# Row maxima of attention scores as y + relu(x - y): one reduction of 1024 or 2 x 512 scores becomes a relu on ScalarE and a fused add and maximum on VectorE

## The reference

```python
scores = einsum('bqhd,bkhd->bhqk', q, k) / sqrt(16)
probs = softmax(scores, axis=-1)          # over 1024 keys
out = einsum('bhqk,bkhd->bqhd', probs, v)
```

## Time and profile before

| what | value |
|---|---|
| median of 3 runs | 438.49 us (438.16 to 438.51) |
| the profiled execution's own time | 436.62 us |
| its span | 434.8 us |
| granted clock of TensorE, mean | 0.985 |
| PE busy | 420.0 us (97%) |
| DVE busy | 370.9 us (85%) |
| ACT busy | 310.1 us (71%) |
| POOL busy | 138.3 us (32%) |

### The profile page before, as it was taken

The page is one execution under the profiler, slowest core; times in us unless marked ns, Lnnn a source line. Parts: engine busy times, 40 slices in busy tenths (PEclk is TensorE's granted clock), DMA queues, the critical chain, the costliest instruction groups (busy, mean ns, idle before and its releaser), DMA issues.

```text
span 434.8 us, 8295 instructions
## 1 busy us (share of the span) xinstructions
PE 420.0 (97%) x3153; PEld 182.1 (42%) x3153; DVE 370.9 (85%) x613; ACT 310.1 (71%) x612; POOL 138.3 (32%) x195
## 2 busy tenths in 40 slices
PE   7999999998999999999999999999999999899993
PEld 3647333333444344444444444444434444333330
DVE  5844798998999999999999999999999999623443
ACT  2231111227889889999999899999989989766882
POOL 7972332444004030511313040322304030401554
PEclk9999999997899999999999999999999999999997
DMA  8949995444000010000000000000000000020002
GB/s 261 310 107 127 133 120 84 62 75 73 4 2 2 21 39 3 2 2 2 4 2 2 2 2 4 2 3 0 3 4 2 3 0 4 3 87 2 21 23 67
DMA packets 13624, 18.09 MB, mean 42 GB/s; under 512 B 3168, under 2 KB 7552, under 8 KB 13584
## 3 DMA queue, kind: packets, MB, share of 16 engines
q1 hardware_dynamic: 12064, 16.44, 20.0%
q10 hardware_dynamic: 1520, 1.12, 0.9%
HBM read 6.72 MB, written 2.10 MB: 20 GB/s over the span
## 4 chain that ended last, share of the span: by engine, by line
PE 86%; POOL 3%; DVE 3%; issue 2%; ACT 2%; DMA 2%; SPq 0%; DVEq 0%; POOLq 0%; ACTq 0%
PE st L1122 32%; PE oT L1090 27%; PE st L934 6%; PE sm L1197 3%; PE oT L1173 3%; PE oT L934 3%; PE sm L1038 2%; PE sm L1013 2%; PE sm L1099 2%; DMA x_sb<-in_x 2%; PE st L1154 2%; PE st L963 2%; POOL arena L466 1%; DVE negmax L795 1%; PE sm L1203 1%
## 5 line engine op out<-in xcount | busy, mean ns | idle before, releaser
L803 DVE TENSOR_REDUCE neghalf<-sm 128x1 f32<-128x512 f32 x448 | 270.9, 680 | 1.5 <-PE sm L1013 1.2
L709 ACT ACTIVATE arena<-st 128x512 f32<-128x512 f32 x448 | 233.0, 600 | 21.1 <-PE st L1122 16.4
L1013 PE MATMUL sm<-kA,qA 48*128 48x512 f32 x448 | 158.1, 446 | 0.0
L1122 PE MATMUL st<-qA,kA 50*128 50x512 f32 x448 | 154.9, 442 | 1.4 <-DVE z_sb L846 1.1
L1090 PE MATMUL oT<-arena,vg 128*32 128x256 f32 (+3 forms) x1568 | 129.7, 423 | 0.0
L1122 PEld LDWEIGHTS st<-qA,kA 50*128 50x128 f32 x448 | 74.0, 186 | 98.7 <-ACT arena L709 82.1
L537 POOL TENSOR_TENSOR rsum<-junk,consts 128x16 f32<-128x16 f32 x13 | 37.9, 2913 | 127.9 <-ACT junk L681 127.9
L1013 PEld LDWEIGHTS sm<-kA,qA 48*128 48x128 f32 x448 | 74.1, 186 | 2.6 <-DVE neghalf L803 2.1
L1090 PEld LDWEIGHTS oT<-arena,vg 128*32 128x32 f32 x1568 | 33.5, 109 | 46.7 <-issue 42.4
L795 DVE TENSOR_REDUCE negmax<-sm 128x1 f32<-128x1024 f32 x32 | 37.9, 1218 | 7.0 <-PE sm L1038 7.0
L730 ACT ACTIVATE arena<-st 128x512 f32<-128x512 f32 x48 | 27.0, 602 | 14.6 <-PE st L1154 14.6
(11 more groups left out here) (122 smaller groups left out, 360.2 us busy)
## 6 DMA issues: line engine op xcount, KB each, us to landing
qA<-arena SPq DMA_DIRECT2D x45, 128.0 KB, 5.1
x_sb<-in_x SPq DMA_DIRECT2D x8, 256.0 KB, 5.8
kA<-qA SPq DMA_DIRECT2D x12, 128.0 KB, 6.6
wT_sb<-in_wT SPq DMA_DIRECT2D x1, 1024.0 KB, 7.5
out<-x_sb SPq DMA_DIRECT2D x1, 896.0 KB, 4.1
out<-x_sb SPq DMA_DIRECT2D x4, 224.0 KB, 2.0
z_sb<-in_wq SPq DMA_DIRECT2D x1, 768.0 KB, 10.0
qA<-qA SPq DMA_DIRECT2D x3, 128.0 KB, 3.8
```

The source lines that it names most:

```text
L709: act.activation(probs[:, s % PB, h, :], st[:, st_score(0, s, h) % 3, :], ACT.Exp, scale=float(D) ** -0.5).then_inc(st_free, 1)
L803: dve.tensor_reduce(neghalf[:, e // 16, e % 16, j % 2:j % 2 + 1], sm[:, n % 4, :], AX.X, ALU.max, negate=True).then_inc(sm_free, count)
L1013: pe.matmul(sm[:, n % 4, :], qA[rows, half, g // 2, h, qt * P:(qt + 1) * P], kA[rows, g // 2, kh * HALF:(kh + 1) * HALF], start=True, stop ...
L1122: pe.matmul(st[:, n % 3, :], kA[rows, g // 2, kt * P:(kt + 1) * P], qA[rows, half, g // 2, h, :], start=True, stop=True).then_inc(st_full, 1)
```

## The change

A row tile's two halves of keys give scores x and y. The kernel after computes the maximum of the two, element by element, as y + relu(x - y). x - y comes from one matmul of the queries with the difference of the two halves of k. ScalarE takes relu of that bank and writes it to SBUF; one VectorE instruction (`tensor_tensor_reduce`) adds it to the bank of y and takes the maximum along the row.

All 32 row tiles of group 0 go this way (`first_relu`, `first_row_max`). In the loop the row tiles that begin at j mod 32 = 12 and 24 do (`BY_RELU`), four of 32 per group; the other 28 are two reductions each, as before.

What comes with it: the differences of k are made by GpSimd (one subtraction, one low part) and ScalarE (one high part), put in place for group 0 by `put_rows("rows of d", 0)` instead of `put_rows("rows of k", 0)`, and brought to `d_rows` by six DMAs. Maxima are kept with their own sign (`row_top`, `half_top`), and the constant rows in `kA` are -1 in place of 1. The relus lie in tiles 4 and 5 of `x_sb`, which two DMAs load again from `x` after the last maximum. `late_gate` and `late_heads` change places. In ScalarE's list the casts, the squares and the tanhs of the mixed stretch are put between the relus.

```diff
+BY_RELU = (12, 24)
+def by_relu(j):
+    return j % 32 in BY_RELU
# ScalarE, mixed stretch
+            def first_relu(e):
+                act.wait_ge(sm_full, 2 * e + 1)
+                if e >= 2:
+                    act.wait_ge(sm_free, 2 * (e - 1))
+                act.activation(relus[:, e % 2, :], sm[:, 2 * e % 4, :], ACT.Relu).then_inc(relu_done, 1)
...
+            for kind, i, rows in MIXED:
+                if kind == "v":
+                    cast(waiting)
+                    waiting = None
+                for r in range(rows):
+                    if r == 2 and waiting is not None:
+                        cast(waiting)
+                        waiting = None
+                    first_relu(entry)
+                    entry += 1
+                    if kind == "q" and i[0] == 3 and r == 1:
+                        gate_tanh_of(i[1])
...
# ScalarE, loop
+            def row_relu(g, j):
+                n = relus_through(g, j) - 1
+                act.wait_ge(sm_full, sm_score(g - 1, j) + 1)
...
+                act.activation(relus[:, n % 2, :], sm[:, sm_score(g - 1, j) % 4, :], ACT.Relu).then_inc(relu_done, 1)
                         act.activation(probs[:, s % PB, h, :], st[:, st_score(0, s, h) % 3, :], ACT.Exp,
                                        scale=float(D) ** -0.5).then_inc(st_free, 1)
+                        if by_relu(4 * s + h - 1):
+                            row_relu(g + 1, 4 * s + h - 1)
# VectorE
+            def top_of_sum(to, bank, n):
+                dve.wait_ge(relu_done, n + 1)
+                return dve.tensor_tensor_reduce(relus[:, n % 2, :], bank, relus[:, n % 2, :], 1.0, LOWEST,
+                                                ALU.add, ALU.max, to)
+            def pair_max(g, j):
+                n, e = sm_score(g, j), j // 2
                 dve.wait_ge(sm_full, n + 2)
+                top_of_sum(half_top[:, e // 16, e % 16, 0:1], sm[:, (n + 1) % 4, :],
+                           relus_through(g + 1, j) - 1).then_inc(sm_free, 1)
...
                 for j in range(64):
                     if j == 33:
                         both_halves(g, 0)
-                    row_max(g, j, 2 if j in (OUT1_AT - 1, OUT0_AT - 1) else 1)
+                    if by_relu(j):
+                        pair_max(g, j)
+                    elif not by_relu(j - 1):
+                        row_max(g, j, 2 if by_relu(j + 1) or j in (OUT1_AT - 1, OUT0_AT - 1) else 1)
# TensorE, loop
+                keys = d_rows[rows, g // 2, :] if by_relu(j) else kA[rows, g // 2, kh * HALF:(kh + 1) * HALF]
...
+                    if i >= 4 and by_relu(i - 4):
+                        pe.wait_ge(relu_done, relus_through(g + 1, i - 4))
                     score_rows(g + 1, i, sm_score(g, i), 2 if first and i == OUT1_AT - 1 else 1)
# GpSimd
+                if (halves[n]) == ("k", 1):
+                    pool.tensor_tensor(difference, rotated_at(0), rotated_at(n), ALU.subtract).then_inc(diff_done, 1)
                 if n < len(halves) - 3:
                     rope_sum(n + 1)
+                if (halves[n]) == ("k", 1):
+                    pool.wait_ge(diff_hi, 1)
+                    pool.tensor_tensor(difference_part(1), difference, difference_part(0).bitcast(F32),
+                                       ALU.subtract).then_inc(diff_lo, 1)
# TensorE, mixed stretch
                 if e == 0:
-                    pe.wait_ge(pj_act, emptied(PJ_AT["rows of k", 1])[1])
+                    pe.wait_ge(pj_act, emptied(PJ_AT["rows of d", 0])[1])
```

More of the change, by code:

```diff
@@ L132, in sm_score, with relus_through @@
     return sm_base(g) + j + (1 if j >= OUT1_AT else 0) + (1 if j >= OUT0_AT else 0)
+def by_relu(j):
+    return j % 32 in BY_RELU
+def relus_through(g, j):
+    return 32 + len(BY_RELU) * (2 * (g - 1) + j // 32) + sum(b <= j % 32 for b in BY_RELU)
 def sm_out1(g):
@@ L608, in cast, with put_k @@
                     act.wait_ge(stacked[n - PART_BUFS], 16 * SLOT_DMAS)
-                act.activation(part(n, 0), rot[:, n % 2, :], ACT.Copy).then_inc(part1, 1)
-            def put_k(i):
-                e = PJ_AT["rows of k", i]
+                act.activation(part(n, 0), rotated_at(n), ACT.Copy).then_inc(part1, 1)
+            def put_k(what, i):
+                e = PJ_AT[what, i]
                 act.wait_ge(pj_full, e + 1)
@@ L623, in put_q, with keep_u @@
                     act.activation(qA[0:ROWS + KR, 0, 0, h, :], pj(e)[0:ROWS + KR, :], ACT.Copy).then_inc(pj_act, 1)
[L625 to L638, removed]
+            def keep_u(hh):
+                e = PJ_AT["u", hh]
+                act.wait_ge(ffn_in, 80)
+                act.wait_ge(pj_full, e + 1)
+                act.activation(uT[:, hh * HALF:(hh + 1) * HALF], pj(e), ACT.Copy,
+                               scale=p_sb[:, 0:1]).then_inc(pj_act, 1)
+            def first_relu(e):
[3 more added lines that the diff above has]
+                act.activation(relus[:, e % 2, :], sm[:, 2 * e % 4, :], ACT.Relu).then_inc(relu_done, 1)
             def gate_tanh_of(t):
@@ L657, in squares @@
                                accum_out=norms[:, t, 0:1]).then_inc(norm_done, 1)
[L659 to L668, removed]
+            for n in range(3):
+                cast(n)
+            put_q()
+            act.wait_ge(diff_done, 1)
+            act.activation(difference_part(0), difference, ACT.Copy).then_inc(diff_hi, 1)
+            cast(3)
+            put_k("rows of k", 1)
+            put_k("rows of d", 0)
+            entry, waiting = 0, None
+            for kind, i, rows in MIXED:
[10 more added lines that the diff above has]
+                        gate_tanh_of(i[1])
+                if kind == "q":
+                    waiting = halves.index((kind, i))
+                elif waiting is not None:
+                    cast(waiting)
+                    waiting = None
+                if kind == "u":
+                    keep_u(i)
+                if kind == "z":
+                    squares(i)
+                if (kind, i) == ("z", 1):
+                    act.wait_ge(pj_full, PJ_AT["max0", 0] + 1)
+                    act.activation(maxT[:, 0, :], pj(PJ_AT["max0", 0]).bitcast(BF16)[0:32, 0:P],
+                                   ACT.Copy).then_inc(pj_act, 1)
             def evacuate(blocks, half, free):
@@ L674, in evacuate @@
                     act.wait_ge(*free)
-                act.activation(heads[:, half, :], oT[:, :], ACT.Copy).then_inc(heads_out, 1)
+                act.activation(heads[half], oT[:, :], ACT.Copy).then_inc(heads_out, 1)
             def copy_turned(n, at):
@@ L969, in put_rows @@
                 n = PJ_AT[kind, i]
-                of = halves.index(("k", i) if kind == "rows of k" else ("q", (0, 0)))
-                column = 0 if kind == "rows of k" else 1 + i
+                column = 1 + i if kind == "rows of q" else 0
                 claim(n)
                 pe.wait_ge(columns_set, 1 + 3 * len(Q_SLOTS))
-                for which, done in ((0, part1), (1, part2)):
-                    pe.wait_ge(done, of + 1)
-                    mm = pe.matmul(pj(n), put_col[:, which, column, :],
-                                   part(of, which), start=(which == 0), stop=(which == 1))
+                for which in range(PARTS):
+                    if kind == "rows of d":
+                        pe.wait_ge((diff_hi, diff_lo)[which], 1)
+                        of_which = difference_part(which)
+                    else:
+                        of = halves.index(("k", i) if kind == "rows of k" else ("q", (0, 0)))
+                        pe.wait_ge((part1, part2)[which], of + 1)
+                        of_which = part(of, which)
+                    mm = pe.matmul(pj(n), put_col[:, which, column, :], of_which, start=(which == 0), stop=(which == 1))
                 mm.then_inc(pj_full, 1)
@@ L1098, in turn_heads @@
                 for t in range(TH):
-                    mm = pe.transpose(bank[:, t * P:(t + 1) * P], heads[:, half, t * P:(t + 1) * P], id_sb[:, :])
+                    mm = pe.transpose(bank[:, t * P:(t + 1) * P], heads[half][:, t * P:(t + 1) * P], id_sb[:, :])
                 return mm
```

101 lines of the change are left out of this document (70 added, 31 removed).

## The result

The kernel after takes 464.21 us (median of 4 runs, 463.81 to 465.42), the kernel before beside it 438.34 us (438.16 to 438.51): ratio 1.0595, 95% interval 1.0574 to 1.0616. The forecast was 457.2 us in a range of 444 to 466. The direction and the kind of loss came out as forecast; the loss is 25.9 us (27.2 between the two profiled executions) where 18.7 were worked out.

The account below looks back on a forecast made before the run. VectorE's row reductions were taken to bound the loop. The profiled 436.62 us plus 18.1 in the loop and 0.6 before it gave 455.3; from the runs' median, 438.49 + 18.7 = 457.2 us, range 444 to 466.

Parts of the forecast that it names:

- The bound: In the loop: VectorE sets the time, 19.4 us per half group; TensorE needs 18.6, so it can regain only 0.8.
- rival (1): In the loop: relus come in time and VectorE's saving counts, half group 18.9 us, total 432 us; chance 0.13.
- T: Start of the first score of a pair's burst in the loop; relu expected at T + 1.51, sum at T + 2.16.
- The price of the sum: In the loop: VectorE's new sum instruction costs 0.74 us per pair, with ends of 0.60 and 0.79.
- The stalls: In the loop: VectorE waits for the relu at a half group's two pairs, 1.00 and 1.31 us; half +1.37 us.
- the hand chain: Estimated durations followed step by step through a half group of the loop: 20.77 us against 19.40.
- D(17): End of position 17's reduction, counted to the next one's start; row score 20 waits for it, until T + 5.31.
- ScalarE's delay: In the loop: the relu delays exps, so the next burst's third score waits 0.39 us; not added to the forecast.
- (2): In the loop: only ScalarE's delay of the third score counts, +0.43 us per half, about 445 us; chance 0.12.
- (3): New sum instruction far dearer, say 1.2 us, or TensorE's clock comes down for a stretch: 465 us and more; chance 0.07.
- (4): Whole kernel: everything cancels, no measurable change; chance 0.04.
- Group 0 and before: Group 0 loses 1.7 us, its gates filling part of the stalls; the stretch before the loop adds 0.6 us.

## Why the prediction was right, and where its sizes were off

**The bound.** VectorE sets the time of the loop: right only as far as a stretch without idle time goes. The run without relu and wait has a half group of 19.30 us where TensorE was put at 18.6 and the loop at 18.9 for rival (1). With VectorE's work less, the loop gives back 0.1 us in 32 positions, not 0.8. This is the first term that was mis-sized.

**The times of relu and sum.** Relu at T + 1.51: measured 1.50 (198.23 - 196.73). VectorE can start the sum at T + 2.16: measured 2.25, as 0.15 us pass between the relu's end and the sum, where the exp's release of TensorE gave 0.06. The price of the sum was taken at 0.74; it is 0.61 to the next operation (199.59 - 198.98), at the low bound of 0.60. Together these two, +0.09 and -0.13 a pair, nearly cancel.

**The stalls.** This is the step that failed in size. Followed they were 1.00 and 1.31 us, bounds 0.9 and 1.4; measured are 1.44 and 1.48, 1.46 in the mean, outside the bounds. VectorE's side of the chain was right: from the second sum's end (207.88) 18 reductions and a join reach position 11's end at 218.81 (220.26 - 1.45), 10.93 us where 10.95 were worked out. TensorE's side was not. The second pair's burst came at T + 8.28 instead of 8.08, and the next half's T at 21.28 instead of 20.77. A T that is later by 0.5 is a relu later by 0.5, and VectorE, on time, waits for it. The half group has 42.76 / 2 = 21.38 us instead of 20.77.

The rows for the second pair and the next half, which this reading uses:

```profile
205.02 0.49 PE L1133 MATMUL sm<-d_rows,qA 48*128 48x512 f32 x1
...
207.26 0.69 DVE L893 CUSTOM_DVE_ANT_0 x_sb<-sm,x_sb 128x512 f32<-128x512 f32 x1 [1.48 <-ACT x_sb L776]
207.88 0.08 DVE L893 DVE_READ_ACCUMULATOR2_ANT half_top<- 128x1 f32 x1
...
218.01 0.50 PE L1133 MATMUL sm<-d_rows,qA 48*128 48x512 f32 x1
...
220.26 0.69 DVE L893 CUSTOM_DVE_ANT_0 x_sb<-sm,x_sb 128x512 f32<-128x512 f32 x1 [1.45 <-PE sm L1133]
```

The term that was too small is the 0.23 us that the hand chain has from a row score that came late to the block of values behind it. It is 0.42 at row score 17 (200.15 - 199.73) and 0.43 at row score 20 (202.55 - 202.12), and the trace of the kernel before has it too, behind the row score of 193.74 in the earlier trace rows:

```profile
194.16 0.85 PE L1090 MATMUL oT<-arena,vg 128*32 128x384 f32 x8
```

Put into the chain in place of 0.23, with nothing else changed, 0.42 counts twice in a half group: behind row score 20 and behind row score 29. Behind row score 17 the wait for D(17) covers it. The second pair's burst then comes at T + 8.27, the two stalls are 1.50 and 1.19, and the half takes 21.15 us, which is 0.38 of the 0.61 that were missing. Of the rest, the longer hand-over from the relu to the sum and from the sum to TensorE (0.14 to 0.15 in place of 0.06) is a part; it was not followed further.

**ScalarE's delay.** The prediction sized it rightly at the third score (0.39; measured 0.40) and left it out, as it "lies beside VectorE's stall". At the burst followed above that is so: the row score behind the late column score waits longer, for the sum's bank. The chain of the prediction, which holds no delay of exps, meets the measured half within 0.23 us once its 0.42 is right. But it would be wrong to count the delay as nothing: as soon as the wait is gone it shows, 1.97 us a group (1.84 with activations that nobody reads). What the wait would cost alone was not run.

**Rivals.** (1), the saving counts, 432 us: its condition falls at once (idle time at the pairs 1.46 us, not under 0.3), and even with all waits gone the kernel would have had 436.6. (2), only ScalarE's delay, 445 us: the mechanism is real and under-sized, 450.9 when measured alone, because it counted 0.45 us of slack that isn't there; and without the wait 1.74 of the 3.94 us a group stay, not the whole. (3): the sum is not dear. The granted clock was 1.00 from 147 to 380 us in both profiles. (4): no.

**Group 0 and before.** Group 0 lost 2.90 where 1.7 stood. Its four sums wait 1.35 us each, so the gates fill next to none of the stall. Even 2.90 is too little, as the granted clock differs between the two profiles. The stretch from 104 to 112 us, before and then after (busy us by engine; the third number from the end is the granted clock, a mean over stretches at full clock and at 0.50, the level of 1.2 GHz):

```profile
104.00:112.00 8.00, 8.00 (x37) 3.01 (x35) 7.47 (x14) 5.19 (x12) 1.37 (x5) 0.57 0.16 20
```

```profile
104.00:112.00 8.00, 7.71 (x39) 2.85 (x39) 8.00 (x14) 5.77 (x13) 1.41 (x6) 0.79 0.30 36
```

In both profiles TensorE had waited for VectorE in front of the loop's first column score, 1.08 and 0.88 us, and the clock fell some us later; it stayed low for longer in the kernel before. So both reach the burst of position 12 at the same time:

```profile
111.35 0.49 PE L1122 MATMUL st<-qA,kA 50*128 50x512 f32 x1
```

```profile
111.35 0.49 PE L1242 MATMUL st<-qA,kA 50*128 50x512 f32 x1
```

The 0.65 us by which the loop began later are gone there, and all that group 0 loses lies behind it: 36.14 us to the group's end (147.49) against 32.59 (143.94), 3.55 more, near the 3.94 of the other groups and twice the forecast. That the 0.65 us agree with 0.6 means little: the stretch before the loop does the same work in all ten experiments' kernels, and their first column score starts between 101.54 and 103.39 us.

**What stays open.** How the 2.20 us a group that the wait adds divide between VectorE's idle time and the bank that comes back late. The relu one exp sooner took 0.45 us off the sum's wait at a pair, gave the bank back sooner too, and brought 1.86 a group; the later sum took 1.65 us of VectorE's idle time out of a group and brought 0.80, with the sum's bank as late as before and another bank delayed too. No version here beats the kernel before.

## What to carry to other kernels

Work moved from the busiest engine to a less busy one is not free because the receiver shows idle time: ask which item of its fixed list stands behind the insertion, and who waits for that item's buffer. Where short rings tie three engines together, two delays can lie one inside the other: the wait that ends last sets the time, and the shorter one shows in full once the longer is taken away, so the parts that a run without each of them shows are not to be added without thought. Take the time from a wait's end to the next work from a row where that wait occurs, not from a row without it; and a saved instruction pays only if no other engine is within that much of the same pace. An experiment that removes the costs and keeps the saving tells first what there is to win, here 0.2 us a group.

## What the runs showed of the hardware

`tensor_tensor_reduce` with one PSUM and one SBUF input of 128x512 appears as `CUSTOM_DVE_ANT_0` of 0.69 us and 0.61 from start to start, nearly what a reduction of 512 elements takes (0.60), though it also writes 512 elements to SBUF. A row `DVE_READ_ACCUMULATOR2_ANT` of 0.08 us stands behind each of them and starts together with the next reduction (both at 199.59): unlike the row of L895, behind which the next operation starts 0.12 us later, it takes no time of its own here. The Trainium skill, "VectorE: DVE Perf Modes", section "Two Vector instructions with no wait between them", calls an operation with an accumulator output two instructions. The trace agrees with the two rows; it shows no price for the second.

A relu of 128x512 out of PSUM costs ScalarE 0.48 us in its row of exps (198.71 - 198.23), about what an exp costs (0.49). With its input in SBUF it has 0.63 us and costs 0.52 (195.27 - 194.75 in the run with unread activations).

A block of values behind a row score that had to wait starts 0.42 to 0.43 us after it (194.16 - 193.74 before; 200.15 - 199.73 and 202.55 - 202.12 after), where a burst whose row score did not wait has 0.33 (190.20 - 189.87 in the earlier trace rows).
